# Second stage of a two-stage attention kernel: the feed-forward layer takes two token tiles at once, and a tile's neurons run two iterations later

## Chip, cores, metric

One Trainium2 chip, one core. The metric is device time in microseconds (us), the median of several executions. Engines: TensorE (PE, its weight loads PEld), VectorE (DVE), ScalarE (ACT), GpSimd (POOL) and SyncE (SP, which issues DMAs).

## What is computed

The input is 4096 tokens (2 x 2048) of 256 values. Four residual layers follow each other, each behind a layer norm:

```
x = x + attn_a(layernorm(x))      # 16 heads of 16, softmax over 2048 tokens
x = x + ffn(layernorm(x))
x = x + attn_b(layernorm(x))      # 16 heads, (b,h,dh,t) reshaped without a transpose
x = x + ffn(layernorm(x))

def ffn(x):
    h = square(relu(x @ W_fc.T))          # 256 -> 1024
    y = h @ W_proj.T                      # 1024 -> 256
    mem = 0
    for step in range(5):                 # spiking neuron; the output is the share of steps with a spike
        reset = mem > 1;  mem = 0.9 * mem + y - reset;  spk = mem > 1
    return mean(spk)
```

The kernel uses that the number of spikes depends on `y` alone: it counts how many of five fixed levels `y` exceeds.

## The kernel before

**Tiles and stages.** The tokens are cut into T = 32 tiles of 128. Stage A runs the first attention and the first feed-forward layer, and projects for the second attention. Stage B runs the second attention and the second feed-forward layer. Both are software pipelines written out by hand: in iteration `it` of stage B the attention scores of tile `it` are made, the attention product of tile `it-1` is finished, tile `it-2` goes through the feed-forward layer, and tile `it-3` gets its spike count and is stored.

**Slots.** An iteration has 32 slots (`c` in the code, two for each head). In a slot PE makes one score tile of 1024 columns (two bf16 matmuls of 512 columns, line 725) into one of three PSUM buffers, DVE takes its negated row maximum (974), ACT takes the exponential into SBUF (1172), and then PE may write that buffer again, three slots on (two at slot 8). Each engine runs its instructions in program order. Everything else is put between the slots by lists of slot numbers. `PROD_AT` places the 16 products of weights and exponentials of an iteration (line 705: four fp32 matmuls of 512 columns side by side in the array, eight in the trace) at slots 0, 6, 7, 9, 10, 12, 13, 15, 16, 22, 23, 25, 26, 28, 29 and 31. `UP_B` places the eight blocks of the first feed-forward matmul ("ups", line 680, each two fp32 matmuls of 128 columns) and `DOWN_B` those of the second ("downs", line 691, each one fp32 matmul of 256 columns). The profile shows two instructions for every fp32 matmul. All of the layer's PSUM results go through one bank, `bank_f`.

**The other engines in the layer.** ACT copies the transposed tile out of PSUM (line 1130), applies relu to each half of the hidden layer (1138) and copies `y` (1143). POOL squares each half in place (1320), counts spikes in ten instructions (1330 to 1338, called `spikes`), adds the residual (`result`, 1346), adds attention and residual for the next tile (1471), and normalises it (1310 to 1315). Between these POOL does small steps of the softmax: `half_distance` (1357), `half_sums` (1364, 1366) and `weigh_q` (1372, 1378). DVE needs the sum of `half_sums` for its reciprocal (965) behind slots 18 and 2. The last tile of a stage is counted on DVE, in six instructions (941 to 948).

**Loop.** `iterations` writes out iterations 1 to 5 of stage B, loops over 6 to 31 two at a time and writes out the drain up to 34.

Of the kernel before, what the change touches and what calls it, by code (L numbers as in the profile page):

```python
# [34 lines left out]
P = 128  # L35
BATCH, SEQ, D = 2, 2048, 256
H, DH = 16, 16
FF = 1024
# [71 lines left out]
def build(nc, x, w_in, b_in_col, b_in_row, w_out, b_out, wq, bq_col, wkv, bkv_row, temp, w_fc, w_proj, out):  # L110
# [9 lines left out]
    with ctx:  # L120
# [88 lines left out]
        xin = sb("xin", [P, 2, D])  # L209
        xout = sb("xout", [P, 2, D])  # L210
        xn = sb("xn", [P, D])
        xnT = sb("xnT", [P, KC, P])
        hid = sb("hid", [P, FF])
        y = sb("y", [P, 2, D])
        pv_sb = hid[:, :].rearrange("p (s d) -> p s d", s=SUB)
        bias_res = hid[0:1, :]
        bias_parts = [n[0:1, :, :].rearrange("o a d -> o (a d)").bitcast(BF16) for n in (y, xin, xout)]
# [46 lines left out]
        ffn_fc, ffn_relu, ffn_sq, ffn_y, ffn_ysb = (sem(n) for n in ("ffn_fc", "ffn_relu", "ffn_sq", "ffn_y", "ffn_ysb"))  # L264
        lif, lif_last, ffn_out = sem("lif"), sem("lif_last"), sem("ffn_out")
# [38 lines left out]
        def last_tile(n):  # L304

            return isinstance(n, int) and n in (T - 1, 2 * T - 1)
# [38 lines left out]


# [9 lines left out]
        def _(sp):  # L356
# [168 lines left out]
            def phase_b(it, par, _):  # L525
# [18 lines left out]
                i = tile_at(it, 3)  # L544
# [5 lines left out]
            iterations(sp, phase_b, (T - 2,))  # L550
# [5 lines left out]
        def _(pe):  # L556
# [109 lines left out]
            def ffn_transpose(n):  # L666
                pe.wait_ge(ffn_xn, n + 1)
                need(pe, ffn_ysb, n)
                if isinstance(n, int) and n == T:
                    pe.wait_ge(qkv_qf, T)  # L670
                transpose2(bank_f, xn).then_inc(ffn_tr, 1)
# [22 lines left out]


# [130 lines left out]
            def phase_b(it, par, _):  # L826
                i, i1, i2 = tile_at(it, 0), tile_at(it, 1), tile_at(it, 2)
                for c in range(CPT):
                    if i is not None:
                        head_scores(i, par, c)  # L830
                    if i2 is not None:
                        if c == 1:
                            ffn_transpose(T + i2)
                        for f in range(FF // P):
                            if c == UP_B[f]:
                                ffn_up(T + i2, f)
                        for f in range(FF // P):
                            if c == DOWN_B[f]:
                                ffn_down(T + i2, f)
# [6 lines left out]
            iterations(pe, phase_b, first=1)  # L846
# [3 lines left out]
        def _(dve):  # L850
# [85 lines left out]
            def last_neuron(n, r, ran, stored, count):  # L936

                y_n = y[:, r, :]
                dve.wait_ge(ffn_ysb, n + 1)
# [8 lines left out]
                v.scalar_tensor_tensor(out=xout[:, r, :], in0=cnt[:, :], scalar=1.0 / STEPS, in1=xin[:, r, :],  # L948
# [84 lines left out]
            def phase_b(it, par, _):  # L1033
                i, i1, i2, i3 = (tile_at(it, n) for n in range(4))
                for c in range(CPT):
                    if i is not None:
                        head_maxima(i, par, c)
                    if i1 is not None:
                        if c == 2:
                            row_rec(i1, 1)  # L1040
                        if c == 24:
                            ffn_stats_of(T + i1, 1 - par, x3_ready, i1 + 1)
                        if c == 25:
                            ffn_mean(T + i1)
                    if c == 22 and i2 is not None and last_tile(T + i2):
                        last_neuron(T + i2, par, 1, out_stored[par], 8 * (i2 - par))
            iterations(dve, phase_b, first=1)
# [3 lines left out]
        def _(act):  # L1051
# [93 lines left out]

            def row_fac(i, half):
# [94 lines left out]
            def phase_b(it, par, _):  # L1241
                i, i1, i2 = tile_at(it, 0), tile_at(it, 1), tile_at(it, 2)
                for c in range(CPT):
# [4 lines left out]
                    if i2 is not None:  # L1248
                        if c == 1:
                            ffn_columns(T + i2)  # L1250
                        if c == 4:
                            ffn_act(T + i2, 0)
                        if c == 13:
                            ffn_act(T + i2, 1)
                        if c == 20:
                            ffn_take(T + i2, par)
            iterations(act, phase_b, first=1)
# [3 lines left out]
        def _(pool):  # L1261
# [60 lines left out]
            def spikes(n, ran, r, first, last):  # L1322
# [4 lines left out]
                for k in range(first, last + 1):  # L1327
                    if k == 1:
                        stand_alone(pool, (ffn_ysb, n + 1), (ffn_out, n))
# [11 lines left out]
            def result(n, ran, r, stored, count):  # L1341
# [4 lines left out]
                g_.tensor_tensor(xout[:, r, :], spk[:, :], xin[:, r, :], ALU.add).then_inc(ffn_out, 1)  # L1346
# [120 lines left out]
            def add_attention(i, par):  # L1467
                pool.wait_ge(x2_loaded, 16 * (i + 1))
                pool.wait_ge(attn_loaded, 16 * 2 * SC * (i + 1))
                need(pool, ffn_out, T + i - 1)  # L1470
                g_.tensor_tensor(xin[:, par, :], x2_in[:, :], attn, ALU.add).then_inc(x3_ready, 1)  # L1471

            def phase_b(it, par, _):
                i, i1, i2, i3 = (tile_at(it, n) for n in range(4))
                if i1 is not None:
                    half_sums(i1, 1 - par, 1)
                if i3 is not None:
                    spikes(T + i3, T - 1 + i3, 1 - par, 7, 8)
                if i1 is not None:
                    weigh_q(i1, 1 - par, 1)  # L1480
                if i3 is not None:
                    spikes(T + i3, T - 1 + i3, 1 - par, 9, LIF_OPS)
                if i2 is not None:
                    square(T + i2, 0)
                if i3 is not None:
                    if isinstance(i3, int) and i3 < 2:
                        pool.wait_ge(x2_stored[1 - par], 16 * T // 2)
                        pool.wait_ge(qkv_xn, T)
                    result(T + i3, T - 1 + i3, 1 - par, out_stored[1 - par], 8 * (i3 - (1 - par)))
                if i2 is not None:  # L1490
                    square(T + i2, 1)
# [53 lines left out]
```

## Time and profile before

| | us |
|---|---|
| median of 3 runs | 2894.28 (2893.46 to 2894.94) |
| profiled execution, its own time | 2899.75 |
| its span, first to last instruction | 2897.9 |
| PE, DVE, ACT, POOL busy in the span | 2429.6, 2508.3, 2555.1, 1311.4 |
| mean granted TensorE clock | 0.959 of full speed |

The profile is one execution with a record of every instruction on every engine. Busy shares add overlapped instructions; matmuls are pipelined, so the distance between starts tells more of PE than their lengths do. Stage B takes the span from about 1450 us on.

### The profile page before, as it was taken

Reading aid. Unit: us, or ns where it says so; the run is one execution under the profiler, and the core shown is the slowest. Engines: PE = TensorE matmul, PEld = TensorE weight load, DVE = VectorE, ACT = ScalarE, POOL = GpSimd, SP = SyncE. Lnnn points to the kernel's source line nnn. Section 1 sums busy time; section 2 is a strip of 40 time slices with the busy share of each in tenths; the row PEclk is TensorE's granted clock in tenths of the full one; section 3 lists DMA queues with packets and bytes.
Section 4 is the critical chain, followed back from the end, with each engine's and each line's share of the span. In section 5 each row is a group of like instructions: output and inputs, shape, how many; then the busy total and the mean of one; then the engine's idle time right before and its main releaser. Section 6 shows DMA issues by size and latency. Waiting matters only on the chain. (4 is left out here: it accounts for less than half of the span.)

```text
span 2897.9 us, 46130 instructions
## 1 busy us (share of the span) xinstructions
PE 2429.6 (84%) x12672; PEld 1067.9 (37%) x12672; DVE 2508.3 (87%) x2584; ACT 2555.1 (88%) x4753; POOL 1311.4 (45%) x1924
## 2 busy tenths in 40 slices
PE   5787878787778777777767999999999999999997
PEld 2344444443334333343332333333333333333333
DVE  5898888899999999999848899888998898899883
ACT  2899889899999999999847899999999999999994
POOL 1247566655445544554441434433443443443344
PEclk8999999899999999999879999999999999999999
DMA  6512121323211111111111011111111101111100
GB/s 200 126 50 65 51 72 44 81 62 80 63 40 31 36 33 40 38 29 33 38 31 50 25 44 41 34 35 40 38 30 43 40 27 42 40 32 37 40 27 13
DMA packets 190808, 139.26 MB, mean 48 GB/s; under 512 B 92163, under 2 KB 177669, under 8 KB 190726
## 3 DMA queue, kind: packets, MB, share of 16 engines
q1 hardware_dynamic: 190726, 138.28, 17.7%
q8 instruction: 37, 0.61, 0.1%
q14 instruction: 45, 0.37, 0.0%
HBM read 92.04 MB, written 41.94 MB: 46 GB/s over the span
## 5 line engine op out<-in xcount | busy, mean ns | idle before, releaser
L974 DVE TENSOR_REDUCE nmax<-score 128x1 f32<-128x1024 f32 x1024 | 1213.9, 1215 | 174.5 <-PE score L725 157.7
L992 DVE TENSOR_REDUCE nmax<-score 128x1 f32<-128x1024 f32 x1024 | 1195.2, 1213 | 145.9 <-PE score L757 141.2
L1172 ACT ACTIVATE big<-score,nmax 128x1024 f32<-128x1024 f32 x1024 | 1138.5, 1118 | 132.6 <-DVE nmax L974 126.2
L1193 ACT ACTIVATE score<-score,nmax 128x1024 f32<-128x1024 f32 x1024 | 1118.8, 1098 | 70.2 <-DVE nmax L992 67.1
L757 PE MATMUL score<-big,shared 128*128 128x512 bf16 x2048 | 640.3, 402 | 256.4 <-ACT score L1193 229.9
L725 PE MATMUL score<-shared 128*128 128x512 bf16 x2048 | 620.4, 390 | 111.0 <-ACT big L1172 83.1
L705 PE MATMUL bank_g<-big,qw 128*32 128x512 f32 x4096 | 546.0, 606 | 2.3 <-POOL qw L1378 1.3
L725 PEld LDWEIGHTS score<-shared 128*128 128x128 bf16 x2048 | 138.7, 98 | 657.5 <-ACT big L1172 520.8
L1320 POOL TENSOR_TENSOR hid<-hid 128x512 f32<-128x512 f32 x128 | 133.0, 1039 | 468.2 <-ACT hid L1138 468.1
L757 PEld LDWEIGHTS score<-big,shared 128*128 128x128 bf16 x2048 | 140.8, 100 | 550.0 <-ACT score L1193 456.3
L680 PEld LDWEIGHTS bank_f<-xnT,w_fc_sb 128*128 128x128 f32 x2048 | 297.2, 199 | 78.1 <-ACT hid L1138 24.4
L680 PE MATMUL bank_f<-xnT,w_fc_sb 128*128 128x128 f32 x2048 | 310.0, 284 | 10.3 <-ACT hid L1138 8.3
L691 PE MATMUL bank_f<-w_proj_sb,hid 128*128 128x256 f32 x1024 | 275.9, 383 | 12.2 <-POOL hid L1320 10.6
L1336 POOL TENSOR_SCALAR spk<-y 128x256 f32<-128x256 f32 x248 | 266.3, 1074 | 26.0 <-POOL cnt L1338 15.2
L691 PEld LDWEIGHTS bank_f<-w_proj_sb,hid 128*128 128x128 f32 x1024 | 191.2, 190 | 81.6 <-ACT hid L1138 13.9
L1193 ACT ACTIVATION_READ_ACCUMULATOR score<-score,nmax 128x1 f32 x1024 | 219.6, 214 | 0.0
L1172 ACT ACTIVATION_READ_ACCUMULATOR big<-score,nmax 128x1 f32 x1024 | 207.7, 203 | 0.0
L1338 POOL TENSOR_TENSOR cnt<-cnt,spk 128x256 f32<-128x256 f32 x248 | 179.9, 725 | 23.3
L705 PEld LDWEIGHTS bank_g<-big,qw 128*32 128x32 f32 x4096 | 81.3, 108 | 219.5 <-issue 217.4
L1310 POOL TENSOR_SCALAR var<-mv 128x1 f32<-128x1 f32 x96 | 22.7, 236 | 237.9 <-DVE mv L934 135.1
L1138 ACT ACTIVATE hid<-bank_f 128x512 f32<-128x512 f32 x128 | 76.9, 600 | 35.8 <-PE bank_f L680 34.2
L1471 POOL TENSOR_TENSOR xin<-x_in,pieces 128x256 f32<-128x256 f32 x32 | 23.4, 731 | 180.4 <-DMA pieces<-shared 141.7
(142 smaller groups left out, 1666.1 us busy)
## 6 DMA issues: line engine op xcount, KB each, us to landing
shared<-q_parts SPq DMA_DIRECT2D x256, 64.0 KB, 2.4
shared<-kb_parts SPq DMA_DIRECT2D x256, 64.0 KB, 2.2
shared<-vb_parts SPq DMA_DIRECT2D x256, 64.0 KB, 2.2
big<-k_parts SPq DMA_DIRECT2D x48, 192.0 KB, 5.1
big<-k_parts SPq DMA_DIRECT2D x24, 256.0 KB, 7.2
kb_parts<-shared SPq DMA_DIRECT2D x96, 64.0 KB, 1.5
vb_parts<-shared SPq DMA_DIRECT2D x96, 64.0 KB, 1.6
shared<-in_x SPq DMA_DIRECT2D x32, 128.0 KB, 2.3
```

The lines of the kernel that those rows point to most:

```text
L680: last = mm(bank_f[:, (f % 4) * P:(f % 4 + 1) * P], w_fc_sb[:, k, f * P:(f + 1) * P], xnT[:, k, :], start=(k == 0), stop=(k == KC - 1))
L691: last = mm(bank_f[:, 0:D], hid[:, f * P:(f + 1) * P], w_proj_sb[:, f, :], start=(f == 0), stop=(f == FF // P - 1))
L705: last = mm(bank_g[32 * sc:32 * sc + 32, :], qw[:, sc * BANK // CH, n, :], expo[:, HALF * half + n, sc * BANK:(sc + 1) * BANK], start=(hal ...
L725: last = mm(score[buf][:, k * BANK:(k + 1) * BANK], bstack[:, par, 0, row:row + P], bstack[:, par, 1, col:col + BANK], start=True, stop=True)
L757: last = mm(score[buf][:, k * BANK:(k + 1) * BANK], qstack[:, par, c // NCH, :], keys[:, b, c // NCH, col:col + BANK], start=True, stop=True)
L974: v.tensor_reduce(nmax[:, par, c // NCH, c % NCH:c % NCH + 1], score[buffers_b[CPT * par + c][0]][:, :], AX.X, ALU.max, negate=True).then_ ...
L992: v.tensor_reduce(nmax[:, par, c // NCH, c % NCH:c % NCH + 1], score[buffers_a[CPT * par + c][0]][:, :], AX.X, ALU.max, negate=True).then_ ...
L1172: a.activation(expo[:, c // NCH, (c % NCH) * CH:(c % NCH + 1) * CH], score[buffers_b[CPT * par + c][0]][:, :], ACT.Exp, bias=nmax[:, par, ...
L1193: a.activation(s[:, :], s[:, :], ACT.Exp, bias=nmax[:, par, c // NCH, c % NCH:c % NCH + 1], accum_out=esum[:, par, c // NCH, c % NCH:c % N ...
L1320: g_.tensor_tensor(h, h, h, ALU.mult).then_inc(ffn_sq, 1)
L1336: ins = g_.tensor_scalar(spk[:, :], y_n, LEVELS[k // 2], 0.0, ALU.is_gt, ALU.add)
L1338: ins = g_.tensor_tensor(cnt[:, :], cnt[:, :], spk[:, :], ALU.add)
```

## The change

The second stage's feed-forward layer works on pairs of tiles. In odd iterations both tiles of a pair are transposed (four transposes in slot 1), and each of the eight weight blocks is applied to 256 columns at once. Relu and square work in quarters that hold both tiles; ACT copies 512 columns where it copied 256, half as often. The 16 downs of a pair (eight for each tile) are spread over slots 24, 27 and 30 of the odd iteration and 13 slots of the even iteration behind it. Spike counting of a tile moves from two or three iterations behind its scores to five (`LIF_LAG`); its ten instructions all run in one iteration and stand at other places among POOL's steps. `xin` grows from two buffers to four. The last two tiles, not one, are counted on DVE. The loop takes four iterations per trip over 8 to 31; 1 to 7 are written out, and the drain runs up to 36.

```diff
-UP_A, UP_B = [18, 19, 20, 21, 22, 23, 24, 25], [4, 4, 5, 5, 8, 11, 14, 14]
-DOWN_A, DOWN_B = [26, 26, 27, 27, 28, 29, 30, 30], [17, 18, 18, 19, 19, 20, 20, 21]
+UP_A, UP_PAIR = [18, 19, 20, 21, 22, 23, 24, 25], [4, 5, 8, 11, 14, 17, 20, 21]
+DOWN_PAIR = [[24, 27, 30], [1, 2, 3, 4, 5, 8, 11, 14, 17, 18, 19, 20, 21]]
+LIF_LAG = 5
...
+            for it in range(1, 8):
+                body(it, it % 4)
+            with eng.Fori(8, cut, 4) as it:
+                for k in range(4):
+                    body(it + k if k else it, k)
+            for it in range(cut, T + LIF_LAG):
+                body(it, it % 4)
...
+            def pair_up(p, f):
+                if f == 0:
+                    pe.wait_ge(pair_xT, p + 2)
+                elif f % 2 == 0:
+                    pe.wait_ge(pair_relu, 2 * p + f // 2)
+                for k in range(KC):
+                    last = mm(bank_f[:, (f % 2) * 2 * P:(f % 2 + 1) * 2 * P], w_fc_sb[:, k, f * P:(f + 1) * P], xnT_both[:, k, :],
+                              start=(k == 0), stop=(k == KC - 1))
...
+            def pair_take(p):
+                act.wait_ge(pair_y, p + 2)
+                act.wait_ge(ffn_out, T + p)
+                a.activation(y[:, :, :], bank_f[:, :].rearrange("p (r d) -> p r d", r=2), ACT.Copy).then_inc(pair_ysb, 2)
...
+                        for n in range(4):
+                            if c == UP_PAIR[2 * n + 1] - 1:
+                                pair_act(up, n)
+                    if down is not None and par == 0 and c == DOWN_PAIR[1][-1] - 1:
+                        pair_take(down)
...
                 if i1 is not None:
                     half_sums(i1, 1 - par, 1)
+                count(1, 2)
                 if i1 is not None:
                     weigh_q(i1, 1 - par, 1)
+                count(3, 4)
+                square_of(0)
+                count(5, 6)
+                square_of(1)
+                count(7, 9)
+                if i is not None:
+                    half_distance(i, par, 0)
+                square_of(2)
+                if i is not None:
+                    half_sums(i, par, 0)
+                count(LIF_OPS, LIF_OPS)
+                if i is not None:
+                    weigh_q(i, par, 0)
...
+                    result(T + n, T - 1 + n, 1 - par, out_stored[1 - par], 8 * (n - (1 - par)), (quad + 3) % 4)
+                square_of(3)
```

On POOL, the order of instructions around the first half's sums, in the loop of the kernel before (`hid` is the square, `dlt` is `half_distance`, `sume` and `tot` are `half_sums`, `wgt` and `qw` are `weigh_q`):

```order
L1320 TENSOR_TENSOR hid<-hid 128x512
L289 ISA
L1346 TENSOR_TENSOR xout<-spk,xin 128x256
L1320 TENSOR_TENSOR hid<-hid 128x512
L1356 ISA
L1357 TENSOR_TENSOR dlt<-nrow,nmax 128x16
L1363 ISA
L1364 TENSOR_TENSOR sume<-esum,fac 128x16
L1365 ISA
L1366 TENSOR_TENSOR tot<-sume 128x8
L1372 TENSOR_TENSOR wgt<-fac,rec 128x16
```

and at the same place of an odd iteration after the change:

```order
L1426 TENSOR_TENSOR cnt<-cnt,spk 128x256
L1444 ISA
L1445 TENSOR_TENSOR dlt<-nrow,nmax 128x16
L1406 REGISTER_ALU
L1408 TENSOR_TENSOR shared<-shared 128x512
L1451 ISA
L1452 TENSOR_TENSOR sume<-esum,fac 128x16
L1453 ISA
L1454 TENSOR_TENSOR tot<-sume 128x8
L299 REGISTER_ALU
L1422 TENSOR_SCALAR spk<-cnt 128x256
L1460 TENSOR_TENSOR wgt<-fac,rec 128x16
```

A square (line 1408, the third quarter) now stands between the distance and the sums, and one counting step between the sums and the weights.

On PE, the loop of the kernel before from slot 8's up to slot 10's product (line 725 is the scores, 680 an up, 705 a product):

```order
L680 MATMUL bank_f<-xnT,w_fc_sb 128x128 x2
L283 REGISTER_ALU
L725 MATMUL score<-shared 128x512 x2
L705 MATMUL bank_g<-big,qw 32x512 x4
L283 REGISTER_ALU
L725 MATMUL score<-shared 128x512 x2
L705 MATMUL bank_g<-big,qw 32x512 x4
```

and the same slots after the change, in an odd iteration and then in an even one (both from the part that is written out; line 787 is the scores, 767 a product, 742 an up of a pair, 753 a down):

```order
L742 MATMUL bank_f<-xnT_pair,w_fc_sb 128x256 x2
L787 MATMUL score<-shared 128x512 x2
L767 MATMUL bank_g<-big,qw 32x512 x4
L787 MATMUL score<-shared 128x512 x2
L767 MATMUL bank_g<-big,qw 32x512 x4
L787 MATMUL score<-shared 128x512 x2
```

```order
L753 MATMUL bank_f<-w_proj_sb,hid 128x256
L787 MATMUL score<-shared 128x512 x2
L767 MATMUL bank_g<-big,qw 32x512 x4
L787 MATMUL score<-shared 128x512 x2
L767 MATMUL bank_g<-big,qw 32x512 x4
L787 MATMUL score<-shared 128x512 x2
```

So slots 8, 11 and 14, which stand alone between products, hold one or two ups of 128 columns before; after, an up of 256 columns in odd iterations and one down in even ones.

At the end of POOL's program, behind the last loop trip and the drain's softmax steps, the kernel before has, from the last normalisation on (`xn`):

```order
L1315 TENSOR_SCALAR xn<-xin,mv,rstd 128x256
L1338 TENSOR_TENSOR cnt<-cnt,spk 128x256
L1336 TENSOR_SCALAR spk<-y 128x256
L1338 TENSOR_TENSOR cnt<-cnt,spk 128x256
L1336 TENSOR_SCALAR spk<-y 128x256
L1338 TENSOR_TENSOR cnt<-cnt,spk 128x256
L1336 TENSOR_SCALAR spk<-y 128x256
L1338 TENSOR_TENSOR cnt<-cnt,spk 128x256
L1334 TENSOR_SCALAR spk<-cnt 128x256
L1320 TENSOR_TENSOR hid<-hid 128x512
L1346 TENSOR_TENSOR xout<-spk,xin 128x256
L1320 TENSOR_TENSOR hid<-hid 128x512
```

and after the change the same stretch begins so, and a second tile's ten counting steps and its `xout` follow it:

```order
L1398 TENSOR_SCALAR xn_pair<-xin,mv,rstd 128x256
L1418 TENSOR_SCALAR cnt<-y 128x256
L1424 TENSOR_SCALAR spk<-y 128x256
L1426 TENSOR_TENSOR cnt<-cnt,spk 128x256
L1424 TENSOR_SCALAR spk<-y 128x256
L1408 TENSOR_TENSOR hid<-hid 128x512
L1426 TENSOR_TENSOR cnt<-cnt,spk 128x256
L1424 TENSOR_SCALAR spk<-y 128x256
L1408 TENSOR_TENSOR hid<-hid 128x512
L1426 TENSOR_TENSOR cnt<-cnt,spk 128x256
L1424 TENSOR_SCALAR spk<-y 128x256
L1426 TENSOR_TENSOR cnt<-cnt,spk 128x256
```

Behind the last `xn`, POOL had eight counting steps, two squares and one result; it has twenty counting steps, four squares and two results.

## Rows read from the trace of the kernel before

**Rows 1.** Busy time by windows, stage B's iterations 6 to 30 (x: instructions).

```profile
core 0: us, PE busy (x) PEld busy (x) DVE busy (x) ACT busy (x) POOL busy (x), PEclk, DMA share, GB/s
1743.70:2810.90 1067.20, 1006.55 (x6054) 364.49 (x6050) 964.67 (x950) 978.88 (x1776) 439.18 (x725) 0.99 0.13 37
```

**Rows 2.** Timeline of PE in one iteration: start us, length us, instruction, idle before.

```profile
2341.67 0.38 PE L561 MATMUL bank_f<-ident,xn 128*128 128x128 f32 x2
...
2343.97 0.60 PE L725 MATMUL score<-shared 128*128 128x512 bf16 x2 [1.35 <-ACT big L1172]
2345.10 0.61 PE L725 MATMUL score<-shared 128*128 128x512 bf16 x2 [0.53 <-ACT big L1172]
...
2347.80 0.59 PE L725 MATMUL score<-shared 128*128 128x512 bf16 x2
...
2349.33 0.60 PE L725 MATMUL score<-shared 128*128 128x512 bf16 x2
...
2351.34 0.60 PE L725 MATMUL score<-shared 128*128 128x512 bf16 x2 [0.41 <-ACT big L1172]
2351.78 0.61 PE L680 MATMUL bank_f<-xnT,w_fc_sb 128*128 128x128 f32 x4
2352.23 0.59 PE L725 MATMUL score<-shared 128*128 128x512 bf16 x2
...
2363.62 0.60 PE L725 MATMUL score<-shared 128*128 128x512 bf16 x2
...
2364.49 0.59 PE L725 MATMUL score<-shared 128*128 128x512 bf16 x2
...
2369.46 0.60 PE L725 MATMUL score<-shared 128*128 128x512 bf16 x2
```

**Rows 3.** Timeline of DVE: first row maxima of iterations 6, 20, 21, 31.

```profile
1743.74 3.48 DVE L974 TENSOR_REDUCE nmax<-score 128x1 f32<-128x1024 f32 x3
...
2341.45 1.22 DVE L974 TENSOR_REDUCE nmax<-score 128x1 f32<-128x1024 f32 x1 [0.44 <-POOL dlt L1357]
...
2383.48 3.49 DVE L974 TENSOR_REDUCE nmax<-score 128x1 f32<-128x1024 f32 x3
...
2810.94 2.36 DVE L974 TENSOR_REDUCE nmax<-score 128x1 f32<-128x1024 f32 x2
```

**Rows 4.** Timeline of ACT in the same iteration: copies among exponentials.

```profile
2344.95 0.37 ACT L1130 ACTIVATE xnT<-bank_f 128x256 f32<-128x256 f32 x1
...
2363.99 1.11 ACT L1172 ACTIVATE big<-score,nmax 128x1024 f32<-128x1024 f32 x1 [0.23 <-DVE nmax L974]
...
2366.62 0.59 ACT L1160 ACTIVATE shared<-bank_g 128x512 f32<-128x512 f32 x1
```

**Rows 5.** Timeline of POOL and DVE around slots 15 to 18.

```profile
2361.44 1.04 POOL L1320 TENSOR_TENSOR hid<-hid 128x512 f32<-128x512 f32 x1 [10.53 <-ACT hid L1138]
...
2364.23 0.20 POOL L1366 TENSOR_TENSOR tot<-sume 128x8 f32<-128x8 f32 x1
...
2366.53 0.19 DVE L965 RECIPROCAL rec<-tot 128x8 f32<-128x8 f32 x1
```

**Rows 6.** Windows at the start of iteration 22: as Rows 1.

```profile
2425.50:2430.00 4.50, 2.63 (x14) 0.85 (x11) 4.06 (x6) 3.85 (x9) 2.61 (x6) 1.00 0.00 0
2430.00:2433.50 3.50, 3.50 (x17) 3.06 (x16) 2.40 (x3) 3.12 (x6) 1.98 (x4) 0.51 0.17 37
```

**Rows 7.** Timeline of POOL and DVE at the end of the span.

```profile
2879.00 1.23 POOL L1315 TENSOR_SCALAR xn<-xin,mv,rstd 128x256 f32<-128x256 f32 x1 [0.17 <-issue]
...
2881.08 1.08 POOL L1336 TENSOR_SCALAR spk<-y 128x256 f32<-128x256 f32 x1 [0.16 <-POOL cnt L1338]
2882.31 0.73 POOL L1338 TENSOR_TENSOR cnt<-cnt,spk 128x256 f32<-128x256 f32 x1
...
2893.10 0.29 DVE L941 TENSOR_SCALAR cnt<-y 128x256 f32<-128x256 f32 x1 [16.77 <-ACT y L1143]
...
2895.27 0.43 DVE L948 SCALAR_TENSOR_TENSOR xout<-cnt,xin 128x256 f32<-128x256 f32 x1
```

More of the change, by code:

```diff
@@ L830, in phase_b @@
                         head_scores(i, par, c)
-                    if i2 is not None:
+                    if up is not None:
                         if c == 1:
-                            ffn_transpose(T + i2)
+                            pair_transpose(up)
                         for f in range(FF // P):
[L835 to L839, printed above, removed]
+                            if c == UP_PAIR[f]:
+                                pair_up(up, f)
+                    if down is not None and c in DOWN_PAIR[1 - par]:
+                        pair_down(down, DOWN_PAIR[1 - par].index(c) + (0 if par else len(DOWN_PAIR[0])))
                     if i1 is not None and c + CPT in PROD_AT[1] and not (isinstance(i1, int) and i1 == 0):
@@ L845, in phase_b @@
                         head_product(i, c)
-            iterations(pe, phase_b, first=1)
+            iterations_b(pe, phase_b)
         @block.vector
@@ L1320, in square, with pair_square, spikes @@
                 g_.tensor_tensor(h, h, h, ALU.mult).then_inc(ffn_sq, 1)
-            def spikes(n, ran, r, first, last):
+            def pair_square(p, n):
+                pool.wait_ge(pair_relu, 2 * p + n + 1)
+                h = hid_pair[n // 2][:, 2 * (n % 2):2 * (n % 2) + 2, :]
+                g_.tensor_tensor(h, h, h, ALU.mult).then_inc(pair_sq, 1)
+            def spikes(n, ran, r, first, last, taken=ffn_ysb, count=None):
                 if last_tile(n):
@@ L1328, in spikes @@
                     if k == 1:
-                        stand_alone(pool, (ffn_ysb, n + 1), (ffn_out, n))
+                        stand_alone(pool, (taken, n + 1 if count is None else count), (ffn_out, n))
                         ins = g_.tensor_scalar(cnt[:, :], y_n, LEVELS[0], 0.0, ALU.is_gt, ALU.add)
@@ L1339, in spikes, with result @@
                     ins.then_inc(lif, 1)
-            def result(n, ran, r, stored, count):
+            def result(n, ran, r, stored, count, slot=None):
                 if last_tile(n):
@@ L1345, in result @@
                 stand_alone(pool, (lif, LIF_OPS * ran + LIF_OPS), (stored, count))
-                g_.tensor_tensor(xout[:, r, :], spk[:, :], xin[:, r, :], ALU.add).then_inc(ffn_out, 1)
+                g_.tensor_tensor(xout[:, r, :], spk[:, :], xin[:, r if slot is None else slot, :], ALU.add).then_inc(ffn_out, 1)
             def spread(ap, m):
@@ L1464, in _, with add_attention @@
             iterations(pool, phase_a, unrolled=UNROLLED)
-            def add_attention(i, par):
+            def add_attention(i, slot):
                 pool.wait_ge(x2_loaded, 16 * (i + 1))
                 pool.wait_ge(attn_loaded, 16 * 2 * SC * (i + 1))
[L1470 to L1474, printed above, removed]
+                if isinstance(i, int) and i < 4:
+                    pool.wait_ge(ffn_out, T - 1 + min(i, 1))
+                else:
+                    pool.wait_ge(ffn_out, T + i - 3)
+                g_.tensor_tensor(xin[:, slot, :], x2_in[:, :], attn, ALU.add).then_inc(x3_ready, 1)
@@ L1475, in phase_b, with count, square_of @@
+            def phase_b(it, quad):
+                i, i1, par = tile_at(it, 0), tile_at(it, 1), quad % 2
+                up, n = up_pair(it, quad), tile_at(it, LIF_LAG)
+                def count(first, last):
+                    if n is not None:
+                        spikes(T + n, T - 1 + n, 1 - par, first, last, pair_ysb, n + 1 + par)
+                def square_of(k):
+                    if up is not None:
+                        pair_square(up, k)
                 if i1 is not None:
@@ new lines, in phase_b @@
+                square_of(0)
[10 more added lines that the diff above has]
+                    weigh_q(i, par, 0)
+                if n is not None:
+                    if isinstance(n, int) and n < 2:
```

138 lines of the change are left out of this document (83 added, 55 removed).

## The prediction

> **What bounds the kernel now.** I read the windows first, for stage B as a whole, then PE's timeline slot by slot, then ACT, DVE and POOL at the places where PE waits, and last the end of the span.
>
> Over iterations 6 to 30 (25 of them in 1067.2 us, 42.7 each) PE is busy 94%, ACT 92%, DVE 90% and POOL 41%, at a clock of 0.99 [rows 1]. No single engine is full; three are nearly so, and only three score buffers stand between them. So a slot costs what the latest of three engines makes it cost, and work taken from one engine counts only in slots where that engine is last. The reader is to see which it is, from starts of score matmuls [rows 2]. A slot with a product takes 1.53 us (2347.80 to 2349.33) and has no idle time: PE bounds it. Slots 8, 11 and 14 stand alone between products. Slot 8, scores and one up, takes 0.89 (2351.34 to 2352.23): 0.44 for the scores and 0.45 for an up of four instructions, 0.11 each. Slot 17, scores and one down, takes 0.87 (2363.62 to 2364.49): 0.43 for two instructions of 256 columns, 0.215 each. PE bounds these too. In slots 2 and 3 PE waits for ACT, 1.35 and 0.53, and at slot 8 again 0.41. ACT bounds the way from slot 1 to slot 8 with its copy and its relu, and from slot 17 to 22 (2363.62 to 2369.46, 5.84) with the copy of the product, 0.59 [rows 2, 4]: slot 22 must wait for the exponential of slot 19, and the copy stands ahead of that.
>
> Two iterations without loss would take 42.03 + 42.48. Iteration 20 is 2341.45 to 2383.48, 42.03 [rows 3]. An iteration that follows the end of a loop trip starts DVE 0.44 late; the profile names POOL's `dlt`, but at 2383.48 no such wait stands though the code is the same, so it is the loop's end, 0.45 with every second iteration. Iterations 6 to 30 hold 12 such ends: 25 x 42.03 + 12 x 0.45 = 1056.2, and 1067.2 was measured (1743.74 to 2810.94) [rows 3]. The missing 11 us I put down to the clock. At the start of iteration 22 PE is busy 2.63 of 4.5 us; then the granted clock is 0.51 for 3.5 us, in a stretch that holds ups [rows 6], the lower level (1.2 GHz). What the engine did before: behind slot 1's transposes, a few score matmuls with waits between. At half speed 3.5 us can lose at most 1.75, so 11 us are at least six such falls; I take nine, at 1.2 each.
>
> **The change, part by part.** A "+" is us per iteration against before.
>
> *Ups, 15 odd iterations (3 to 31).* An up on a pair is four instructions of 256 columns. The trace shows that shape as a down: 0.215 each, so 0.87 an up [rows 2]. A pair's 32 instructions take 6.9 us; the 64 for two tiles took 64 x 0.11 = 7.1. PE saves almost nothing, since time follows columns here and the weight load is already hidden. But places change. Slots 8, 11 and 14 held one, one and two ups (0.89 + 0.89 + 1.33 = 3.11) and now hold 3 x 1.31 = 3.93: +0.82. Slots 24 and 27 get a down; part was idle there: +0.18. The copy of the transposes is 512 columns, 0.59 as the product's copy, for 0.37 [rows 4], on ACT's chain to slot 8: +0.2.
>
> *The square ahead of the sums.* The third relu (0.6 as the product's copy) runs on ACT behind slot 16's exponential, which starts at 2363.99 [rows 4] and ends at 2365.1; relu to 2365.7, square (1.04) to 2366.85, two small sums to about 2367.5. DVE takes the reciprocal at 2366.53 and had the sum ready since 2364.43 [rows 5], 2.1 us of cover, which is now spent: it would come at 2367.55. DVE's queue behind it holds slot 19's maximum (1.22 long [rows 3]: to 2368.95), for which its exponential waits (1.11 [rows 4]: to 2370.05), and for that slot 22's scores: 2370.15 instead of 2369.46, +0.7. The low end for this is 0 (POOL early), the high end 1.0.
>
> Sum: 1.9 x 15 = +28.
>
> *Iterations without ups, 15 (2 to 30).* Slots 8, 11, 14 hold one down: 3 x 0.87 = 2.61 for 3.11: -0.50. ACT has no copy and no relu up to slot 8, and DVE's chain of maxima (3.49 for three [rows 3]) takes over as the bound: -0.35. Slots 17 to 22 hold one down each where two stood, but the product's copy on ACT bounds them as before: 0. Slots 24 to 30: 0. Sum: -0.85 x 15 = -13.
>
> *Loop.* Five ends of trips for 12: 7 x 0.45 = -3.
>
> *Clock.* The falls come in even iterations, behind a loop's end, where slots 2 to 4 hold only scores. There each slot now has a down of 0.43 beside the 0.44 of scores. In odd iterations slots 2 and 3 stay bare, but four transposes (some 0.7 for 0.38 [rows 2]) stand ahead, and no loop's end comes before them. I take all falls as gone: the 11 us worked out from rows 3, and one fall more before iteration 6: -12. Bounds 0 and -12. The Trainium skill ("TensorE: Matmul & The Clock Gate", Part 4) says that transposes do not count as PE being busy. The rows here do not settle it: iteration 20 has the same matmuls in these slots as 22 [rows 2] and loses nothing [rows 3]. By the rule the falls would move to odd iterations, the second rival.
>
> *The end.* Counting now comes after the last normalisation, and ACT may copy y of the last pair only when tile 29 is counted (`ffn_out` at T + 30). Behind the last `xn`, which ends at 2880.2 [rows 7] and now some 1.6 earlier (two counting steps no longer stand ahead), POOL has two tiles of ten steps: 5 x 1.23 + 4 x 0.89 + 0.5 = 10.2, a result of 0.8 each, and four squares of 1.1 [rows 5, 7]: 2878.6 + 20.4 + 1.6 + 4.4 + about 1 of waiting for relus = 2906. Then the copy of y (0.6), two tiles on DVE at 2.6 (2893.10 to 2895.70 [rows 7]) and 2.2 for the store as now (2895.7 to 2897.9): 2914.2, **+16.5**.
>
> **Sum:** 28 - 13 - 3 - 12 + 16.5 = +16.5. The profiled execution took 2899.75 (5.5 over the median), the change of the sum is put on the median: 2894.3 + 16.5 = **2911**.
>
> **Rivals.**
> 1. *Forecast*, 2911, with 2902 to 2919 for itself: 0.60.
> 2. *The clock still falls*, now in odd iterations, where slots 2 and 3 are bare. For it: PE was idle 1.35 and 0.53 there [rows 2]. Against: more transposes, no loop's end. 2911 + 12 = 2923: 0.12.
> 3. *The square finds cover*: POOL or DVE is late for another reason. 15 x 0.7 less: 2900.5: 0.10, half of it within 0.2% of before.
> 4. *Faster: even iterations run ahead.* With 37 us of work for PE (16 x 1.53 + 13 x 0.87 + 3 x 0.44) and little on ACT, they could fall to what DVE needs, about 38 us (its 38.5 busy of 42.7), -4 and not -0.85. Against it: a buffer is free only three slots on, so time lost in product slots is not made up. It decides from -1.95 an iteration on (16.5 / 15 more). Half way, -2.5, gives 2886: 0.09.
> 5. *A pass over 256 columns costs little more than one over 128*: ups at 0.45 for a pair give slots 8, 11, 14 2.67, 1.26 less: 15 x 1.26 = 19, 2892, no change. Against it stand 0.11 and 0.215 in rows 2: 0.06. The Trainium skill (same page, "Back-to-back issue gap") gives a sustained spacing of 81 ns at 128 columns and 131 ns at 512, far from proportional. By that rule the pair's ups would save PE over a third of their time.
> 6. Anything else, about no change: 0.03.
>
> **From these to the numbers.** A measurement here tells about 0.2% (5.8 us) from no change. Faster: rival 4, 0.09. Same: 5, 6 and half of 3, 0.14. Slower: the rest, 0.77. The range must reach rival 3 below and 2 above: 2897 to 2925, which leaves out rivals 4 and 5 and the upper edge of 2.
>
> **What would show it.** Ups at 0.215 an instruction; slots 8, 11, 14 at 1.31 in odd and 0.87 in even iterations; odd iterations near 43.9, even ones near 41.2; the reciprocal of slot 18 waiting for POOL in odd iterations alone; clock 1.00 from 1700 us on; more than 15 us between the last `xn` and the last copy of `y`. It is wrong if odd iterations stay under 43, if half clock shows in each of them, if even iterations fall under 40.5, or if the end grows by less than 12 us.

## The result, and the profile after

| | before | changed |
|---|---|---|
| median | 2893.87 us (2887.59 to 2894.94, 4 runs) | 2932.86 us (2931.72 to 2942.41, 4 runs) |
| profiled execution, its span | 2899.75, 2897.9 | 2932.08, 2930.3 |

The change makes the kernel slower: the ratio is 1.0134, 95% interval 1.0116 to 1.0152. That is 39 us by the medians and 32.4 between the two profiled spans. The forecast was 2911 us, 16.5 more than before. Its sign was right; the time lies outside its range.

The windows of stage B's iterations 6 to 30, as [rows 1] (x: instructions):

```profile
core 0: us, PE busy (x) PEld busy (x) DVE busy (x) ACT busy (x) POOL busy (x), PEclk, DMA share, GB/s
1740.80:2823.70 1082.90, 986.80 (x5544) 325.19 (x5642) 968.59 (x951) 979.59 (x1750) 435.91 (x723) 1.00 0.13 38
```

The stretch takes 15.7 more than in [rows 1]. PE's clock is now 1.00 and its busy time is 20 lower, so nothing that fills an engine explains it. Where the time goes is seen from iteration to iteration. DVE's timeline at its first row maxima of iterations 20, 21, 22 and 31, as [rows 3]:

```profile
2349.48 3.49 DVE L1039 TENSOR_REDUCE nmax<-score 128x1 f32<-128x1024 f32 x3 [3.52 <-PE score L787]
...
2390.60 3.49 DVE L1039 TENSOR_REDUCE nmax<-score 128x1 f32<-128x1024 f32 x3
...
2434.31 1.22 DVE L1039 TENSOR_REDUCE nmax<-score 128x1 f32<-128x1024 f32 x1
...
2823.76 2.36 DVE L1039 TENSOR_REDUCE nmax<-score 128x1 f32<-128x1024 f32 x2
```

Iteration 20, even, takes 41.12 (2349.48 to 2390.60); iteration 21, odd, takes 43.71. Both steps were forecast nearly so (41.2 and 43.9). But iteration 20 begins with DVE having stood idle for 3.52. Iteration 19 is the last of a loop trip and took 47.85. The timeline of all engines at another such end, between iterations 11 and 12:

```profile
1995.09 1.21 DVE L1039 TENSOR_REDUCE nmax<-score 128x1 f32<-128x1024 f32 x1
1995.21 1.11 ACT L1255 ACTIVATE big<-score,nmax 128x1024 f32<-128x1024 f32 x1 [0.33 <-DVE nmax L1039]
...
1997.97 0.60 PE L787 MATMUL score<-shared 128*128 128x512 bf16 x2 [2.20 <-ACT big L1255]
...
1999.82 2.43 DVE L1039 TENSOR_REDUCE nmax<-score 128x1 f32<-128x1024 f32 x2 [3.23 <-issue]
...
2001.08 1.11 ACT L1255 ACTIVATE big<-score,nmax 128x1024 f32<-128x1024 f32 x1 [3.43 <-DVE nmax L1039]
```

The last column matters: DVE stood idle for 3.23 in front of slot 0's maximum, and the profile names no one it waited for ("issue": it waited for nothing that the profile shows). Its two score matmuls had started at 1997.97, and a maximum starts some 0.6 behind them elsewhere. PE itself was late too: `big` was free when ACT's exponential ended at about 1996.3, and PE went on at 1997.97. The five ends of trips (iterations 11, 15, 19, 23, 27) took 47.12, 47.42, 47.85, 46.99 and 46.85 against 43.72 for an odd iteration without one.

At the same time the page's list of queues has instruction packets that the kernel before had not. First before, then after (packets, MB, share of the 16 engines' span):

```profile
q8 instruction: 37, 0.61, 0.1%
q14 instruction: 45, 0.37, 0.0%
```

```profile
q8 instruction: 88, 1.44, 0.2%
q14 instruction: 107, 0.88, 0.1%
```

In the stretch 1830 to 2860 the list of queues of the kernel before shows no instruction packet at all; that of the changed kernel does:

```profile
q1 hardware_dynamic: 28251, 36.71, 12.6%
q8 instruction: 52, 0.85, 0.3%
q14 instruction: 65, 0.53, 0.2%
```

In the changed kernel they come trip by trip. The trip of iterations 12 to 15 (1999.8 to 2174.5):

```profile
q8 instruction: 9, 0.15, 0.3%
q14 instruction: 11, 0.09, 0.2%
```

Each of the three trips behind it, to 2697.1, has 9 and 11 again. So the loop of two iterations was fetched once, and the loop of four is fetched again on every trip.

PE in slots 8 and 9 of iteration 21, for [rows 2]:

```profile
2400.70 0.60 PE L787 MATMUL score<-shared 128*128 128x512 bf16 x2 [0.44 <-ACT big L1255]
2401.15 1.03 PE L742 MATMUL bank_f<-xnT_pair,w_fc_sb 128*128 128x256 f32 x4
2402.01 0.59 PE L787 MATMUL score<-shared 128*128 128x512 bf16 x2
```

The ups of a pair take 0.86 (2401.15 to 2402.01), the slot 1.31, both as forecast: a pass over 256 columns costs what two over 128 do, and rival 5 is out.

POOL and DVE around slot 18 of an odd iteration, as [rows 5]:

```profile
2502.04 1.04 POOL L1408 TENSOR_TENSOR shared<-shared 128x512 f32<-128x512 f32 x1 [2.79 <-ACT shared L1221]
...
2503.04 0.22 POOL L1452 TENSOR_TENSOR sume<-esum,fac 128x16 f32<-128x16 f32 x1
...
2503.34 0.20 POOL L1454 TENSOR_TENSOR tot<-sume 128x8 f32<-128x8 f32 x1
...
2503.57 0.20 DVE L1030 RECIPROCAL rec<-tot 128x8 f32<-128x8 f32 x1 [0.55 <-POOL tot L1454]
```

DVE waits 0.55 for the sum behind the square, in odd iterations alone, and slot 18 takes 1.89 for 1.24.

The end, as [rows 7]:

```profile
2921.29 0.72 POOL L1434 TENSOR_TENSOR xout<-spk,xin 128x256 f32<-128x256 f32 x1
2922.13 0.60 ACT L1227 ACTIVATE y<-bank_f 128x512 f32<-128x512 f32 x1 [13.08 <-POOL xout L1434]
2922.76 0.29 DVE L1006 TENSOR_SCALAR cnt<-y 128x256 f32<-128x256 f32 x1 [30.38 <-ACT y L1227]
...
2927.62 0.42 DVE L1013 SCALAR_TENSOR_TENSOR xout<-cnt,xin 128x256 f32<-128x256 f32 x1
```

ACT waits 13.08 for POOL's count of tile 29 before it may copy the last `y`. From iteration 31's first maximum to the end of the span it is 106.5 (2823.76 to 2930.3); before it was 87.0.

### The profile page after: what moved, and what is told of

Same layout as the page of the kernel before. It is cut to its first block and busy times, and to the rows that moved or that the text cites. A ratio compares the mean times of both kernels' runs of the same rounds, so it can differ in the third digit from the quotient of the medians.

```text
span 2930.3 us, 44272 instructions
## 1 busy us (share of the span) xinstructions
PE 2398.2 (82%) x11936; PEld 1022.6 (35%) x12160; DVE 2515.3 (86%) x2590; ACT 2557.3 (87%) x4721; POOL 1301.0 (44%) x1913
## 3 DMA queue, kind: packets, MB, share of 16 engines
HBM read 92.04 MB, written 41.94 MB: 46 GB/s over the span
## 5 line engine op out<-in xcount | busy, mean ns | idle before, releaser
L819 PE MATMUL score<-big,shared 128*128 128x512 bf16 x1959 | 622.6, 405 | 268.9 <-ACT score L1276 234.8
L787 PE MATMUL score<-shared 128*128 128x512 bf16 x1913 | 588.5, 388 | 153.7 <-ACT big L1255 102.3
L1445 POOL TENSOR_TENSOR dlt<-nrow,nmax 128x16 f32<-128x16 f32 x64 | 14.0, 218 | 356.7 <-DVE nrow L1023 356.7
L708 PE MATMUL bank_f<-xnT_pair,w_fc_sb 128*128 128x128 f32 x1024 | 159.0, 278 | 7.7 <-ACT hid L1204 7.7
L708 PEld LDWEIGHTS bank_f<-xnT_pair,w_fc_sb 128*128 128x128 f32 x1024 | 147.3, 191 | 47.2 <-ACT hid L1204 23.5
L719 PE MATMUL bank_f<-w_proj_sb,hid 128*128 128x256 f32 x512 | 140.4, 386 | 10.7 <-POOL hid L1403 9.0
L742 PE MATMUL bank_f<-xnT_pair,w_fc_sb 128*128 128x256 f32 x512 | 134.4, 387 | 2.8 <-ACT hid L1221 1.4
L719 PEld LDWEIGHTS bank_f<-w_proj_sb,hid 128*128 128x128 f32 x512 | 94.1, 190 | 52.2 <-issue 12.8
L742 PEld LDWEIGHTS bank_f<-xnT_pair,w_fc_sb 128*128 128x128 f32 x512 | 96.8, 192 | 32.6 <-ACT xnT_pair L1215 6.7
```

Of the source, the lines that this page charges most:

```text
L708: last = mm(bank_f[:, (f % 4) * P:(f % 4 + 1) * P], w_fc_sb[:, k, f * P:(f + 1) * P], xnT[:, k, :], start=(k == 0), stop=(k == KC - 1))
L719: last = mm(bank_f[:, 0:D], hid[:, f * P:(f + 1) * P], w_proj_sb[:, f, :], start=(f == 0), stop=(f == FF // P - 1))
L742: last = mm(bank_f[:, (f % 2) * 2 * P:(f % 2 + 1) * 2 * P], w_fc_sb[:, k, f * P:(f + 1) * P], xnT_both[:, k, :], start=(k == 0), stop=(k = ...
L787: last = mm(score[buf][:, k * BANK:(k + 1) * BANK], bstack[:, par, 0, row:row + P], bstack[:, par, 1, col:col + BANK], start=True, stop=True)
L819: last = mm(score[buf][:, k * BANK:(k + 1) * BANK], qstack[:, par, c // NCH, :], keys[:, b, c // NCH, col:col + BANK], start=True, stop=True)
```

## The experiments

All comparisons are with the kernel before on the same chip; its median there was 2896.8 to 2898.3, so ratios are the better measure (0.001 is 2.9 us). "Written out" means without a loop.

**e1: the kernel before, with the changed kernel's trips.** Same work, other loop.

```diff
-            iterations(pe, phase_b, first=1)
+            iterations_b(pe, phase_b)        # the same on all engines
...
+            for it in range(1, 8):
+                body(it, it % 2, 0)
+            with eng.Fori(8, cut, 4) as it:
+                for k in range(4):
+                    body(it + k if k else it, k % 2, 0)
```

> The kernel before, with stage B's loop alone changed to the shape that the pair kernel has: 1 to 7 written out, then trips of four iterations over 8 to 31. The loop theory (in the pair kernel DVE sat idle 3.2 us with no wait at the end of a trip, and the instruction queues moved more than twice the packets) expects five late ends of trips at about 3.9 us each for twelve at 0.45: +12 to +17 us against the kernel before. The rival, that the late slot belongs to the pair's own waits, expects -3 us, as in my prediction.

Measured: 2903.27 us, ratio 1.0017 (1.0007 to 1.0027), +5: between the two theories. The trace separates what the time mixes. DVE at the end of iteration 15:

```profile
2124.07 3.49 DVE L985 TENSOR_REDUCE nmax<-score 128x1 f32<-128x1024 f32 x3
...
2169.19 1.23 DVE L985 TENSOR_REDUCE nmax<-score 128x1 f32<-128x1024 f32 x1 [2.96 <-issue]
```

Iteration 15 takes 45.12 where an undisturbed one takes 42.05. The five ends cost 15.7 together, 3.1 each; the 12 ends of before cost 5.4. So +10.3. But the clock falls to half only at the ends of trips, five times for nine, and the iterations behind these ends are late by 1.2, 0.7, 1.2, 0.2 and 0.6 (3.9 together) where nine falls had cost 10.9: -7.0. Together that is +3.3, of the +3.7 between the first maxima of iterations 2 and 31; the rest of the +5 stands outside these. The loop theory had the mechanism and left out the falls that go with fewer ends.

**e2: the changed kernel, written out.**

```diff
-            with eng.Fori(8, cut, 4) as it:
-                for k in range(4):
-                    body(it + k if k else it, k)
-            for it in range(cut, T + LIF_LAG):
+            for it in range(1, T + LIF_LAG):
                 body(it, it % 4)
```

> The pair kernel with stage B written out from iteration 1 to 36, no loop. The loop theory expects the five late ends gone (3.5 us each beyond an ordinary odd iteration, 17.6 in all) and perhaps some of the 5 us of late slots 24: 2910 to 2916 us. The rival (the pair's own waits) expects no change, 2933.

Measured: 2912.26 us, ratio 1.0050 (1.0037 to 1.0063); the span is 24.7 shorter than the changed kernel's. DVE's first maxima of iterations 20, 21 and 22:

```profile
2335.03 1.22 DVE L1034 TENSOR_REDUCE nmax<-score 128x1 f32<-128x1024 f32 x1
...
2376.27 3.48 DVE L1034 TENSOR_REDUCE nmax<-score 128x1 f32<-128x1024 f32 x3
...
2419.85 1.22 DVE L1034 TENSOR_REDUCE nmax<-score 128x1 f32<-128x1024 f32 x1
```

Iterations take 41.24 and 43.58, with no end of a trip among them; beyond that only 14 and 18 are late by more than half a microsecond, at slot 24 (0.9 and 0.6). The loop theory holds.

**e3: the kernel before, written out.** The same edit to its loop.

> The kernel before with stage B written out, no loop. Twelve ends of trips at 0.45 go: -5. If the falls of the clock hang on the late slot behind a trip's end, as I said in the prediction, they go too, up to 11 us more in a profiled execution: -10 to -16. If they do not, -5 alone, with half clock still at starts of iterations.

Measured: 2883.84 us, ratio 0.9946 (0.9933 to 0.9959): **faster than both kernels.** From DVE's timeline, iterations 20 and 21:

```profile
2334.21 3.48 DVE L980 TENSOR_REDUCE nmax<-score 128x1 f32<-128x1024 f32 x3
...
2376.15 3.48 DVE L980 TENSOR_REDUCE nmax<-score 128x1 f32<-128x1024 f32 x3
```

Every undisturbed iteration takes 41.94, odd or even. From iteration 4 to 31 the clock never falls, where it fell nine times before. Iterations 12, 13 and 22 to 24 are about 1 late each, at slot 24, so not all of the 16 us arrive. Against this kernel the pair written out costs 28 us: (43.59 + 41.24 - 2 x 41.94) x 15 = 14, and its end, without what iteration 31 has of these, 16.4; the late iterations of e3, more than e2 has, take some 3 back.

**e4: the third square behind the weighing.**

```diff
-                square_of(2)
                 if i is not None:
                     half_sums(i, par, 0)
                 count(LIF_OPS, LIF_OPS)
                 if i is not None:
                     weigh_q(i, par, 0)
+                square_of(2)
```

> The pair kernel with the third square moved behind the sums and the weights of the first half, nothing else. My step says that the square holds DVE's reciprocal behind slot 18 in each of 15 odd iterations, 0.6 to 0.7 us each: -9 to -10 us against the pair kernel, about 2923, with slot 18 at 1.24 us instead of 1.89. The rival, that another engine is as late there, expects no change.

Measured: 2933.84 us, ratio 1.0120 (1.0105 to 1.0135), not to be told from the changed kernel. The expected 9 to 10 us are not there. DVE in iteration 21:

```profile
2391.68 3.49 DVE L1039 TENSOR_REDUCE nmax<-score 128x1 f32<-128x1024 f32 x3
...
2417.95 0.19 DVE L1030 RECIPROCAL rec<-tot 128x8 f32<-128x8 f32 x1
2418.06 4.81 DVE L1039 TENSOR_REDUCE nmax<-score 128x1 f32<-128x1024 f32 x4
...
2435.20 1.23 DVE L1039 TENSOR_REDUCE nmax<-score 128x1 f32<-128x1024 f32 x1
```

The wait is gone, and slot 19 begins 26.38 into the iteration for 27.02. But the iteration takes 43.52, only 0.19 less. The starts of DVE's maxima show slots 20, 21 and 22 at 1.20, 1.29 and 1.53 where they were 1.13, 1.13 and 1.29: 0.47 of the 0.64 is given back. Behind POOL's wait stood PE: from 2419.93 on, slot 21's scores, its timeline has no idle time: an up, the scores of slot 22, a product, and so on. The square costs 0.2 an iteration, not 0.7.

**e5, e6: whose jump is it?** Only the loops differ: in e5 DVE alone is written out, in e6 all others are.

```diff
-            iterations_b(dve, phase_b)
+            iterations_b(dve, phase_b, straight=True)     # e5; in e6 sp, pe, act and pool instead
```

> The changed kernel with only VectorE's program of stage B written out without a loop; the four other engines keep their trips of 4 iterations. Theory (each engine pays for its own jump back, and VectorE's is the one that is waited for): at 1999.82 VectorE has stood idle for 3.23 us with nothing to wait for, while ScalarE and TensorE wait for what comes out of it. Without its loop the ends of trips keep what the others' own jumps cost (idle times put down to issue of 0.4 to 1.3 at TensorE), so 3.5 an end becomes 0.5 to 1.5: five ends give 10 to 15 back, 2918 to 2923. Rival (the jump of another engine, TensorE or ScalarE, is as late as VectorE's, or all share one supply of instructions): the ends stay at 3 or more, 2929 to 2934.

> The reverse: SyncE, TensorE, ScalarE and GpSimd written out without a loop, VectorE alone with trips of 4 iterations. Theory (VectorE's own jump costs the 3.2 us): ends of trips stay 3.2 to 3.5 over an undisturbed odd iteration, 2929 to 2934. Rival (another engine's jump, or all together): most of it goes, 2912 to 2918.

Measured: e5 2926.86 us, ratio 1.0105 (1.0088 to 1.0121), between its two ranges; e6 2936.05 us, 1.0136 (1.0120 to 1.0152), 2 above the theory's range. In its ends e6 came as the theory said (2.9 to 3.5 each): written out everywhere but on DVE, nothing is won. DVE in e6 behind iteration 11, then PE and DVE in e5 at the same place:

```profile
2001.93 2.36 DVE L1043 TENSOR_REDUCE nmax<-score 128x1 f32<-128x1024 f32 x2 [2.94 <-PE score L791]
```

```profile
1998.67 0.60 PE L791 MATMUL score<-shared 128*128 128x512 bf16 x2 [2.08 <-ACT big L1259]
...
1999.38 1.22 DVE L1043 TENSOR_REDUCE nmax<-score 128x1 f32<-128x1024 f32 x1 [2.05 <-PE score L791]
```

In e6 the profile puts DVE's 2.94 down to the score, which had started at 1999.64 and was long done: the releaser named is not the cause. In e5 DVE is at once behind PE, but PE is late. The five ends cost 10.0 over an undisturbed odd iteration, where they cost 17.6, so 7.7 was won and not the 10 to 15 expected. PE's own jump had been hidden under DVE's.

**e9: DVE and PE written out.**

> The changed kernel with VectorE and TensorE written out in stage B; SyncE, ScalarE and GpSimd keep their trips of 4 iterations. Theory (each engine pays for its own jump; with VectorE written out TensorE's is next: it starts the first score of a trip at 1998.67, 2.08 after its last work, where in the kernel written out entirely it goes on after 0.84): the ends go to under 0.5 and the time to that of the kernel written out, 2912 (2909 to 2917). Rival (ScalarE's or GpSimd's jump is as late as TensorE's): the ends keep 1.0 to 1.9 over an undisturbed odd iteration, 2917 to 2925.

Measured: 2919.41 us, ratio 1.0069 (1.0055 to 1.0083): by time that is the rival's (2917 to 2925). Iterations 11, 15, 19, 23 and 27 now take 43.53, with no end visible. But iterations 12, 16, 20 and 24 take 42.6 for 41.3, and 28 takes 43.79: it has a fall of the clock as well. DVE, ACT and PE at the start of iteration 12:

```profile
2001.19 1.22 DVE L1043 TENSOR_REDUCE nmax<-score 128x1 f32<-128x1024 f32 x1
...
2004.36 1.11 ACT L1259 ACTIVATE big<-score,nmax 128x1024 f32<-128x1024 f32 x1 [1.95 <-DVE nmax L1043]
...
2005.62 0.60 PE L791 MATMUL score<-shared 128*128 128x512 bf16 x2 [1.72 <-ACT big L1259]
```

DVE's maximum of slot 0 was done at 2002.41. ACT's exponential of slot 0 starts at 2004.36, 3.17 behind DVE's start; in e2 at the same place it is 1.61 (1994.27 and 1995.88). PE then waits 1.72 for ACT to free slot 0's buffer. A third engine had a lateness of its own, worth 1.3 an end, under the other two. That it is ACT's jump is read from this place; ACT alone was not written out.

**e7: the last four tiles counted on DVE, not two.**

```diff
-            return isinstance(n, int) and n in (T - 1, 2 * T - 2, 2 * T - 1)
+            return isinstance(n, int) and n in (T - 1, 2 * T - 4, 2 * T - 3, 2 * T - 2, 2 * T - 1)
```

> The changed kernel with the last four tiles (not two) counted on VectorE, so that ScalarE's copy of the last pair's y waits no longer for GpSimd's counting of tile 29 (13.08 us of waiting before it, at 2922.13 in the profile after). Theory (the end is bound by GpSimd's counting): the copy comes when its downs are done, some 2916.5; VectorE has two more tiles at 2.6 to do, in a stretch where it waits; the end is 5 to 6 earlier: 2927, within 2924 to 2929. Rival (GpSimd's squares and relus of the last ups set it anyway, or VectorE's four tiles in a row do): no gain, 2931 to 2934, or up to 5 later.

Measured: 2929.28 us, ratio 1.0113 (1.0098 to 1.0127), against the changed kernel's 1.0134; the two intervals overlap, so the time alone does not settle it. Its profiled span is 2930.5, as long as that of the changed kernel, which is misleading: stage B began 5.5 later in it, and stage A was not touched. From iteration 31's first maximum to the end it is 101.0 for 106.5, the 5.5 expected. ACT's copy now waits for the downs:

```profile
2922.37 0.60 ACT L1227 ACTIVATE y<-bank_f 128x512 f32<-128x512 f32 x1 [7.31 <-PE bank_f L753]
```

**e8: e2, e4 and e7 together.**

> All that helped the pair together: stage B written out without a loop, the third square behind the weighing, the last four tiles counted on VectorE. If the effects add: 2912.3 (written out) less 5.6 (the end) less 15 x 0.18 = 2.7 (the square, from its profile: slot 18 gave 0.64 back and slots 20 to 22 took 0.47) = 2904, within 2900 to 2908: still slower than the kernel before by 0.2 to 0.5% and 20 us slower than the kernel before written out (2883.8). Rival (with no loop the end or the square is covered by something else): 2909 to 2913.

Measured: 2901.9 us, ratio 1.0019 (1.0007 to 1.0030). The effects add. The best pair is still slower than the kernel before, and 0.7% slower than e3.

**e10: half of the ups' work left out in slots 8, 11 and 14**, on e2.

```diff
-                for k in range(KC):
+                steps = 1 if f in (2, 3, 4) else KC
+                for k in range(steps):
...
-                              start=(k == 0), stop=(k == KC - 1))
+                              start=(k == 0), stop=(k == steps - 1))
```

> The pair's kernel written out without a loop, in which the ups of slots 8, 11 and 14 leave out the second half of their contraction (two instructions of 256 columns for four; a part of the computation is left out). Theory (in these slots TensorE's ups set the pace): they fall from 1.30 to 1.14, the slots of a product behind them from 1.53 to 1.27, the odd iteration from 43.59 by about 1.0; 15 x 1.0 off 2912 is 2897 (2893 to 2901). Rival (ScalarE's chain of the copy and the relus sets the way there, or the slots behind take it back, as with the square): under 0.3 an iteration, 2908 to 2913.

Measured: 2892.88 us, ratio 0.9983 (0.9974 to 0.9992), 19 less than e2 and at the lower edge of the theory's range. DVE's first maxima of iterations 21 and 22:

```profile
2366.76 3.48 DVE L1035 TENSOR_REDUCE nmax<-score 128x1 f32<-128x1024 f32 x3
...
2409.14 1.22 DVE L1035 TENSOR_REDUCE nmax<-score 128x1 f32<-128x1024 f32 x1
```

The odd iteration takes 42.38 for 43.58. PE's work in these three slots became 1.3 shorter and the iteration 1.2: nearly all of it lies on the path, the opposite of the square.

## Why the prediction was wrong, by its own steps

Forecast and measured, in us of the profiled span. Measured values come from the starts of DVE's maxima; they add up to the 32.4.

| step | forecast | measured | how |
|---|---|---|---|
| odd iterations | +28 | +25.4 | 43.72 for 42.03, x 15 |
| even iterations | -13 | -13.5 | 41.13 for 42.03, x 15 |
| loop | -3 | +12.2 | 17.6 in five ends for 5.4 in twelve |
| clock | -12 | -11.0 | nine falls of 1.21 (10.9) and 1.4 in iteration 3 gone; 0.7 in iteration 2 and 0.6 in 12 new |
| late slot 24 | none | +2.4 | +5.1 in iterations 10, 14, 18, 22, 26, 30; -2.7 in 2 and 3, where before had it |
| the end | +16.5 | +17.9 | 106.5 for 87.0, less iteration 31's 1.7 |
| start of iteration 2 | none | -1.0 | 1570.6 for 1571.6 |

**The step that failed is the loop**: "Five ends of trips for 12: 7 x 0.45 = -3". It took 0.45 as the price of an end of any trip, read from trips of two iterations, and let the count alone change. The change also doubled what stands inside the loop, with a fetch on each trip. An end then costs 3.5 (3.2 at the jump, in slot 31, and 0.3 in a late slot 24 of the same iteration), 15 us that the forecast does not have. e2 gives these 15 back, e1 shows the same price (3.1) without the pair, e5, e6 and e9 show that it is not one joint pause: DVE and PE are each late by their own amount, and the latest one counts; for ACT this is read from e9's rows alone. That instruction fetch is the cause is inferred from the packets, which come in the traces with long trips and not in that with short ones, and from e1 against before. In code written out they come too (82 on q8 in e3's profile) and cost no such stop. Why a jump back can't be fetched ahead as straight code is, no run here shows. Without the 15 us the time would lie near 2918, inside the range. None of the signs of being wrong that the prediction named appeared: none of them watched the loop.

A rule of the Trainium skill bears on this ("Advanced Engine Details and Errata", section "ISA Cache"), and the forecast should have weighed it: it gives an engine 32 KB for instructions (TensorE 128 KB), with cache lines of 16 KB or 256 instructions, and only two of them. The traces agree in part: a packet on q8 is 16.5 KB (0.61 MB in 37), but one on q14 is 8.2 KB (0.37 MB in 45). DVE's loop body has 155 instructions in the program of before and 307 in the changed one and in e1. By the page's figures, as an estimate, the first lies in at most two such lines, and the second can reach over three. How the rule would give PE, with its larger store, the 2.0 of e5 is not settled here. No run here changed the size of a body in finer steps, so the limit itself is not measured.

**Late slot 24** was not foreseen. DVE waits there for POOL's `xin`, and POOL for SP's transfer of the attention's pieces. After, iteration 19:

```profile
2335.87 0.73 POOL L1562 TENSOR_TENSOR xin<-x_in,pieces 128x256 f32<-128x256 f32 x1 [2.05 <-DMA pieces<-shared]
...
2336.63 0.43 DVE L991 BATCH_NORM_STATS2 st<-xin 128x6 f32<-128x256 f32 x1 [0.55 <-POOL xin L1562]
```

In all it stood there 5.7 us in 11 cases by the list of waits, and 1.8 in 4 cases in e2. Part of the 11 cases lies in the five ends of trips. It thus goes partly with the loop, but not alone: the kernel before had it in iterations 2 and 3 (0.8 and 1.9), and e3, without a loop, in five iterations. What makes SP late was not tried.

**The odd iterations** came out within 0.2 for two reasons that cancel. The ups and their copy cost 1.5 and not 1.2: slots 9 and 12, which hold a product, grew from 1.27 to 1.53, since they had used the time that PE was ahead. The square cost 0.2 and not 0.7 (e4). The step "slot 22's scores at 2370.15 instead of 2369.46" let POOL's lateness run through to the end of the iteration and did not ask who would be last there without it.

**The even iterations** are right, with their mechanism: slots 8, 11 and 14 take 1.14, DVE's and ACT's pace (the 0.87 named among the signs is what PE has in them). Rival 4, an even iteration that runs ahead, is out. **The end** is right by its mechanism (e7), and 1.4 over; its own terms add up to 2914.0, not 2914.2, which changes nothing.

**The clock** is near in amount (11.0 for 12), but its reason is only half right. The falls hang on the ends of trips: gone from iteration 4 on in e3, where slots 2 to 4 are as bare as before. The downs alone don't hold the clock either. e6 has them and falls at all five ends. There DVE alone is late, and PE first runs ahead and then stands. Windows of e6 across the start of iteration 12, and of the changed kernel across that of iteration 16:

```profile
2000.80:2005.30 4.50, 1.23 (x7) 0.66 (x6) 3.37 (x3) 1.75 (x3) 2.07 (x2) 1.00 0.01 4
2005.30:2008.80 3.50, 3.50 (x10) 2.00 (x9) 2.60 (x4) 3.18 (x7) 2.86 (x5) 0.51 0.08 19
```

```profile
2173.40:2177.90 4.50, 3.06 (x16) 1.56 (x12) 3.40 (x3) 2.14 (x3) 1.89 (x2) 1.00 0.01 4
2177.90:2181.40 3.50, 3.15 (x15) 1.26 (x18) 3.50 (x6) 3.50 (x8) 2.86 (x5) 1.00 0.07 19
```

In e6 PE was busy 1.23 of 4.5 and the granted clock then fell to its lower level, 1.2 GHz; in the changed kernel it was busy 3.06 of 4.5 and the clock stayed. But how busy PE was does not alone tell a fall from none. The changed kernel ahead of its one fall at a trip's end, in that fall, and at another end, behind which the clock stayed at 1.00:

```profile
1994.50:1999.00 4.50, 2.30 (x19) 0.43 (x18) 1.97 (x3) 2.82 (x7) 1.24 (x4) 1.00 0.05 11
1999.00:2002.40 3.40, 3.40 (x14) 1.44 (x7) 2.43 (x2) 1.32 (x3) 1.55 (x2) 0.50 0.02 5
2518.40:2522.90 4.50, 2.42 (x20) 0.43 (x18) 2.15 (x3) 3.00 (x7) 1.06 (x4) 1.00 0.05 11
```

The clock stayed behind 2.42 of 4.5 here and fell behind 2.63 of 4.5 in the kernel before [rows 6]. What decides between the two is not shown. Rival 2, falls in the odd iterations with their four transposes, did not come: no odd iteration from 3 on is at half clock but for 0.8 us at the end of iteration 11.

**The remaining 6.6 us** between 32.4 by spans and 39 by medians belong to no step. The profiled execution of before, 2899.75, lies above all four of its timed runs (median 2893.87), and the later comparisons gave before medians of 2896.8 to 2898.3, with 2890 to 2903 as extremes. Part of e7's span shows how such scatter arises in a stage that isn't touched.

## What to carry to other kernels

The price of a loop's end grew here with the size of the body (two sizes were tried), so it can't be carried over from a shorter body: before making a body longer, count its instructions, look whether the profile has instruction packets inside the loop, and price a jump that must be fetched by itself, engine by engine. Removing one wait pays only down to the next one in the same slots, so ask who would be last without it (0.2 of 0.7 here for the square; 1.2 of 1.3 for the ups, where nobody else was near). Work for two tiles at once saves PE nothing where time follows the columns, and it takes more places at once and makes the end of the pipeline longer.

## What the runs showed of the hardware

- The end of a loop trip cost 0.45 us with two iterations in the body and 3.1 to 3.5 with four, in the same kernel and in the changed one. No instruction packets came between 1830 and 2860 us in the first case; some 120 came in the second.
- Each engine pays by itself. With all in loops DVE stood 3.2; with DVE written out PE was the late one, 2.0 an end; with both written out 1.3 was left (read as ACT's).
- The same program without a loop had instruction packets all the way and no such stops, and was 0.5% faster than the tuned loop.
- Matmul time followed columns: 0.11 a pass at 128 and 0.215 at 256 (fp32, two instructions each).
- In e6 a wait of 2.94 was put down to a matmul that had ended about 1.7 earlier. The true cause was an engine's own next instruction, which the profile shows as "issue" only in some of the cases.
